# Opening and tail of a fused attention and mixture-of-experts kernel: first pairs' maxima by an accumulated product, keys of the first batch stored first, second block's attention reordered, last scatters unblocked

## The reference, cut to what matters

```python
# x: (4, 1024, 256), ctx: (4, 77, 256)
q = split(layernorm(x) @ W_q.T + b_q); k, v = split(ctx @ W_k.T + b_k), split(ctx @ W_v.T + b_v)
x = x + tanh(g0) * (merge(softmax(q @ k.T / 4) @ v) @ W_o.T + b_o)
h = layernorm(x) * ln_g + ln_b
top_vals, idx = top_k(h @ Wr, 2);  gates = softmax(top_vals)
shared = (silu(h @ W1s) * (h @ W3s)) @ W2s
# expert e takes its first 732 tokens, in order of choice and token
routed[t] += gate * ((silu(xe @ W1[e]) * (xe @ W3[e])) @ W2[e])
out = x + tanh(g1) * (routed + shared)
```

## Time and profile before

| | |
|---|---|
| median of 3 runs | 852.79 us (852.49 to 857.55) |
| the profiled execution | 850.94 us |
| its span | 849.2 us |
| TensorE busy | 97% of the span |

### The profile page before, as it was taken

One profiled execution on the slowest core, in us unless ns is written; L12 is line 12 of the kernel. 1 busy time (PEld: TensorE's weight loads), 2 busy tenths in 40 slices (PEclk: granted clock), 3 DMA queues, 4 the chain that ended last, 5 costly groups with the idle time before them and its releaser, 6 DMA issues.

```text
span 849.2 us, 14564 instructions
## 1 busy us (share of the span) xinstructions
PE 821.0 (97%) x5228; PEld 719.8 (85%) x5228; DVE 588.6 (69%) x1260; ACT 386.2 (45%) x660; POOL 321.6 (38%) x250
## 2 busy tenths in 40 slices
PE   8888999999999999999999999999999999999995
PEld 7474868868868688687788899999999999999995
DVE  7577788787788777888877666565656756566442
ACT  4547263373453633734445454453544545354331
POOL 7453103150032230303126405818275481834336
PEclk9999999999999999999999999999999999999998
DMA  8541411324104223130032624334444324431112
GB/s 265 136 125 28 125 38 35 90 53 119 19 25 124 43 52 85 34 100 14 26 125 53 194 75 108 71 83 105 110 88 88 102 46 112 98 76 17 16 25 38
DMA packets 92257, 67.24 MB, mean 79 GB/s; under 512 B 53556, under 2 KB 78984, under 8 KB 92200
## 3 DMA queue, kind: packets, MB, share of 16 engines
q1 hardware_dynamic: 39608, 54.79, 23.1%
q0 software_dynamic: 51744, 10.67, 8.8%
q10 hardware_dynamic: 848, 1.05, 0.5%
HBM read 37.75 MB, written 14.27 MB: 61 GB/s over the span
## 4 chain that ended last, share of the span: by engine, by line
PE 81%; DVE 4%; issue 3%; ACT 1%; POOL 1%; DVEq 0%; POOLq 0%; ACTq 0%
PE bank L1692 20%; PE bank L1694 20%; PE bank L1693 20%; PE bank L1993 3%; PE bank L1994 3%; PE bank L1995 3%; PE bank L1832 2%; PE bank L1826 2%; PE bank L1793 2%; PE bank L2035 1%; PE bank L1931 1%; PE bank L2019 1%; PE bank L1699 1%; PE bank L1922 1%; PE bank L1700 1%
## 5 line engine op out<-in xcount | busy, mean ns | idle before, releaser
L1692 PE MATMUL bank<-split_operands 128*128 128x366 f32 (+4 forms) x1104 | 364.9, 331 | 1.6 <-POOL split_operands L972 0.9
L1694 PE MATMUL bank<-split_operands 128*128 128x366 f32 (+4 forms) x1104 | 359.6, 326 | 0.0
L1693 PE MATMUL bank<-split_operands 128*128 128x366 f32 (+4 forms) x1104 | 359.5, 326 | 0.0
L1692 PEld LDWEIGHTS bank<-split_operands 128*128 128x128 f32 (+1 forms) x1104 | 205.8, 186 | 17.7 <-issue 5.9
L1694 PEld LDWEIGHTS bank<-split_operands 128*128 128x128 f32 (+1 forms) x1104 | 205.5, 186 | 10.6
L1693 PEld LDWEIGHTS bank<-split_operands 128*128 128x128 f32 (+1 forms) x1104 | 206.0, 187 | 8.1
L1084 POOL DMA_INDIRECT out<-float_data,scatter_now x42 | 120.1, 2860 | 170.1 <-DVE float_data L1655 146.7
L1675 DVE TENSOR_TENSOR hidden<-bank,float_data 128x366 f32<-128x366 f32 x112 | 60.5, 540 | 108.3 <-PE bank L1694 108.0
L1270 ACT ACTIVATE float_data<-bank 128x366 f32<-128x366 f32 x112 | 53.5, 477 | 110.2 <-PE bank L1694 110.2
L1267 ACT CAST split_operands<-hidden 128x366 fp32r<-128x366 f32 x112 | 55.7, 497 | 68.5 <-DVE hidden L1675 68.5
L1046 POOL DMA_INDIRECT float_data<-z_scratch,gather_now x42 | 72.9, 1736 | 17.6 <-issue 16.1
(11 more groups left out here) (177 smaller groups left out, 1116.1 us busy)
## 6 DMA issues: line engine op xcount, KB each, us to landing
float_data<-in_L_ffn_W SPq DMA_DIRECT2D x21, 1024.0 KB, 7.8
split_operands<-split_operands SPq DMA_DIRECT2D x92, 128.0 KB, 2.4
float_data<-in_x SPq DMA_DIRECT2D x8, 512.0 KB, 4.4
z_scratch<-float_data SPq DMA_DIRECT2D x8, 512.0 KB, 3.1
out<-float_data SPq DMA_DIRECT2D x7, 512.0 KB, 2.9
split_operands<-split_operands SPq DMA_DIRECT2D x8, 192.0 KB, 3.8
float_data<-in_L_ffn_W1s SPq DMA_DIRECT2D x2, 512.0 KB, 9.4
float_data<-in_L_ffn_W3s SPq DMA_DIRECT2D x2, 512.0 KB, 7.6
```

The costliest lines, as they stand in the source:

```text
L1692: pe.matmul(o, lhs[0], rhs[0], start=first, stop=False)
L1693: pe.matmul(o, lhs[0], rhs[1], start=False, stop=False)
L1694: return pe.matmul(o, lhs[1], rhs[0], start=False, stop=last)
```

## The change

It has four places.

**Opening, block 0.** Pairs 0 and 1 get their scores from two products into the same bank: one over the 96 rows of queries and keys, one of a constant `neg` (16 rows, -1 for the own head) with `mtr` itself. They don't wait for `mtr` to be broadcast by DMA. `neg` is made by GpSimd near the start. The key store is cut into the 77 columns of batch 0 and the rest, under two semaphores. ScalarE issues all eight DMAs of the queries' high parts, where SyncE issued four. The transposition of block 1's `xn` stands behind `first_scores`, and VectorE makes both of its parts. `scale_x` of block 1 stands behind `values_out`. Pieces 4 and 5 of the shared weights stand behind `scores(b, 1)`, high and low part.

**Block 0's z and block 1's z.** ScalarE makes the full value too (`full`), VectorE only subtracts (`low_z`); in block 0 VectorE does so behind both reductions of block 1's maxima.

**Block 1's attention.** VectorE scales block 2's `xn` behind the first half of the normalisation, not ahead of it. Its transposition stands ahead of `up(3)`, which stands ahead of the projection. `project_second` orders the projection's matmuls by what is ready: high parts of tiles 0 to 2, then their low parts, then tile 3. Four of six `keep_busy` matmuls go. An activation with no use for its result puts the table for Silu in place early. `up(6)` and `down(4)` are cut into parts around the maxima.

**Tail.** GpSimd no longer waits for `rows_gathered` in `rows_of_last`; VectorE's own wait for it stays.

```diff
     do("stack_maxima", b)
-    do("shared_hi", 2, 3)
+    do("values_out")
     do("scale_x", n)
-    do("shared_lo", 0, 1)
-    do("values_out")
-    do("shared_lo", 1, 6)
+    do("shared_lo", 0, 4)
...
+    do("shared_hi", 2, 3)
+    do("shared_lo", 4, 6)
...
-    nxt("scale_x")
     do("hidden", f, 2)
     nxt("keys")
     do("scores", b, 0)
+    nxt("scale_x")
     do("scores", b, 1)
+    do("silu_table")
+    nxt("transpose_x")
     up(3)
     do("attention_hi", b)
-    nxt("transpose_x")
     do("project", b)
...
             for j in range(2):
-                sp.dma_start(kscr[j].rearrange("(k p) t -> p k t", p=P), k_s[:, j].bitcast(F32)).then_inc(sig["k_stored"], 16)
+                sp.dma_start(kscr[j, :, 0:SK].rearrange("(k p) t -> p k t", p=P), k_s[:, j, :, 0:SK].bitcast(F32)).then_inc(sig["k0_stored"], 16)
+            for j in range(2):
+                sp.dma_start(kscr[j, :, SK:].rearrange("(k p) t -> p k t", p=P), k_s[:, j, :, SK:].bitcast(F32)).then_inc(sig["k_stored"], 16)
...
+            do(pool.memset(neg.bitcast(F32), 0.0))
+            first = neg.rearrange("p a b t -> p (a b) t")
+            pool.affine_select(out=first, in_=first.bitcast(F32), compare_op=ALU.not_equal, fill=-1.0, base=0,
+                               pattern=[[-1, 4], [0, SK]], channel_multiplier=1).then_inc(sig["neg_ready"], 1)
...
-            pool.wait_ge(sig["rows_gathered"], 16 * (NR // 2))
...
+        def full(b, k):
+
+            if b.at(1):
+                act.wait_ge(sig["hl_ready"], b.n * KD + k)
+            act.activation(full_of(b, k), bank[z_bank(b) + k][:, :], ACT.Identity, bias=lnb[:, k:k + 1],
+                           scale=lng[:, k:k + 1]).then_inc(sig["hf_ready"], 1)
...
         def transpose_x(b):
+            if b.at(1):
+                for k in range(KD):
+                    dve.wait_ge(sig["xT_ready"], KD + k + 1)
+                    dve.tensor_copy(xT[:, 0, k], bank[xT_bank(b) + k][:, :]).then_inc(sig["xh_ready"], 1)
...
         def pair_scores(b, p):
             for w in range(2):
+                if b.at(0) and p < 2:
+                    pe.matmul(bank[2 * (p % 2) + w][0:SK, :], kst[0:96, p, w, :], qst[0:96, p, :], start=True, stop=False)
+                    mm = pe.matmul(bank[2 * (p % 2) + w][0:SK, :], neg[:, p, w, :], mtr[:, :], start=False, stop=True)
+                    continue
...
+        def project_second(b):
...
+            pe.wait_ge(sig["ah_ready"], (b.n + 1) * KD)
+            high(0)
+            pe.wait_ge(sig["xl_ready"], (b.n + 2) * KD)
+            for t in (1, 2):
+                high(t)
+            pe.wait_ge(sig["al_ready"], (b.n + 1) * KD)
+            for t in range(3):
+                low(t)
+            pe.wait_ge(sig["x1_ready"], b.n * TT + 1)
+            high(3)
+            low(3)
```

More of the change, by code:

```diff
@@ L205, in second_period @@
     nxt("maxima", 1)
-    up(6)
+    do("up_a", f, 6)
+    down(4, 0, 1)
     nxt("maxima", 2)
-    down(4)
+    do("up_b", f, 6)
+    down(4, 1, 2)
     nxt("maxima", 3)
     do("pick", b, 1)
+    down(4, 2, TT)
     down(5)
@@ L1889, in project_first, with high, low @@
                     mm.then_inc(sig["oproj_ready"], 1)
+        def project_second(b):
+            aT, w = q_of(b), [wat[:, j, 3] for j in range(2)]
+            out = [bank[project_bank(b, t)][:, 0:D] for t in range(TT)]
+            at = [slice(t * P, (t + 1) * P) for t in range(TT)]
+            def high(t):
+                for k in range(KD):
+                    for j in range(2):
+                        pe.matmul(out[t], aT[:, 0, k, at[t]], w[j][:, k], start=(k + j == 0), stop=False)
+            def low(t):
+                for k in range(KD):
+                    mm = pe.matmul(out[t], aT[:, 1, k, at[t]], w[0][:, k], start=False, stop=(k == KD - 1))
+                mm.then_inc(sig["oproj_ready"], 1)
+            pe.wait_ge(sig["ah_ready"], (b.n + 1) * KD)
[9 more added lines that the diff above has]
+            low(3)
         def project(b):
```

79 lines of the change are left out of this document (49 added, 30 removed).

## The result

The changed kernel took **857.09 us** (median of 20 runs, 855.72 to 861.78), the kernel before 852.52 (20 runs, 850.52 to 860.12): a ratio of 1.0049, 95% interval 1.0031 to 1.0067. It is 4.6 us slower, where 3.2 us faster was forecast, and outside the range. The profiled execution took 855.82 us with a span of 854.1.

A forecast was written before the change was run, and what follows sets the result against it. TensorE, busy 821.0 of 849.2 us, was taken as the bound, leaving 28 us to gain. Terms +1.0 - 2.7 - 0.3 - 1.2 = -3.2 us gave 849.6 against the median of 852.79, range 846.8 to 854.5.

The forecast's parts named there:

- 2.8 us later, at 25.0: Opening: the keys' last load, issued near 22.2, lands at 25.0, so first scores start 3.3 us earlier than 28.29.
- the 0.15 us for the added issues ahead of four casts: Opening: ScalarE's four added DMA issues, 2.8 us, delay `mtr` by only 0.15 us, to 24.35.
- The four added matmuls double a row of 1.15 us to 2.3: Opening, first scores on TensorE: the added matmuls take the row from 1.15 to 2.3 us.
- the clock's fall at z alone: Rival, chance 0.22: TensorE's clock falls before block 0's z, costing 3.0 us more, 852.6 us in all.
- The norm starts at 51.1: Block 0, GpSimd: late pieces delay the loads of W2s, so the norm starts 0.9 us later than before.
- late weights: Rival, chance 0.10: loads of W2s take 7.6 us, not 3.9, and the clock's 3.0 come on top: 856.3 us.
- the rival by which GpSimd isn't the bound: Chance 0.12: loads land in 3 us, pieces run through, the norm starts near 49: 847.5 us in all.
- Net -2.7 us: Block 1, up to 87.18: idle time and `keep_busy` go, less short waits; -2.7 us, bounds -1.5 and -3.6.
- -0.3 behind it: `up(6)` and `down(4)` in parts let two reductions pass under matmuls: -0.3 us, bounds 0 and -0.5.
- -0.6, not -5: Tail: VectorE's last result sets the last scatter, at 840.7 instead of 841.34, though the first adding scatter starts 5 us earlier.
- -1.2 in sum: Tail: 0.6 us from the last scatter's earlier start, another 0.6 from faster landing, bounds 0 and 1.6.
- The opening was put at +1.0: Sum up to behind block 0's norm: 1.0 us slower, bounds -1.5 and +5.

The follow-up runs named there:

- e1: Changed kernel with SyncE again issuing four of the eight DMAs of the queries' high parts: 857.58 us, ratio 1.0048.
- t1: Kernel before with only the tail's edit, GpSimd not waiting for `rows_gathered`: 851.46 us, ratio 1.0000.
- t4: Kernel before with only ScalarE issuing all eight DMAs of the queries' high parts: 851.94 us, ratio 0.9997.
- g1: Kernel before with block 1's and the tail's edits and all eight DMAs of the queries' high parts on ScalarE: 847.08 us, ratio 0.9901.
- t2: Kernel before with only block 1's edits, the full value of z on ScalarE, and `up(6)` and `down(4)` cut: 850.00 us, ratio 0.9972.
- t3: Kernel before with block 1's and the tail's edits, so the change without its opening: 848.31 us, ratio 0.9942.
- e2: Changed kernel with seventeen `keep_busy` matmuls ahead of the first scores instead of three: 854.45 us, ratio 1.0005.
- e4: Changed kernel with seventeen `keep_busy` matmuls ahead of the first scores and pieces 4 and 5 ahead of the attention: 848.62 us, ratio 0.9940.
- e3: Changed kernel with pieces 4 and 5 of the shared weights ahead of the attention, as before: 851.76 us, ratio 0.9975.
- g3: e4 with the separate `neg` product taken away, pairs 0 and 1 waiting for the broadcast again: 847.25 us, ratio 0.9910.
- h3: Changed kernel with only the separate `neg` product taken away, `keep_busy` and pieces as they were: 853.79 us, ratio 1.0006.

## Why the prediction was wrong

**Which views were right.** That four waits stand where the profile shows them, and that each edit takes its wait away, held. The forecast fell on what takes their place in the opening.

**"Lands 2.8 us later, at 25.0": failed.** The keys were costed from rows in which nothing else ran beside them. Three things added up to 27.72: the opening was 0.5 us late from `neg` (costed at nothing), the six issues took 5.57 us instead of 4.3, and the last landed 3.15 us behind the end of its issue. e1 shows that 1.9 us of it are from ScalarE's added transfers beside them. `mtr` was there at 25.5, not 24.35: the 0.15 us for the added issues ahead of four casts was 0.7. The wait of 0.7 us for the store is gone, but that is no gain of the edit: without it t1, t4 and g1 start the loads at 18.4 to 18.6, and t2 and t3 at 19.1.

**"The four added matmuls double a row of 1.15 us to 2.3": failed, and it was the costly step.** It assumed the clock of the earlier trace rows. I placed the clock's fall at z alone and gave it 0.22; it came at both places. Eight matmuls took 5.07 us, the transposition 1.6. The change also leaves three of eight `keep_busy` matmuls ahead of the scores and none of the four behind them, to which I gave no price (e2, with seventeen ahead, takes back 2.6 us). The argument against a fall, that the level had stayed at 1.00 through 1.44 and 1.48 us of idle time, was from one execution: t1 shows the same opening with the level at 0.50. The Trainium skill (TensorE: Matmul & The Clock Gate, Part 1: The HAM clock gate) says that an idle TensorE loses half its rate. The trace agrees: 1.8 us into the 2.89 us without a matmul the level went from 1.00 to 0.50. An idle TensorE doesn't account for the falls of e1, e4 and t2, which came while it was busy.

**"The norm starts at 51.1": right in its mechanism, and well sized.** From the end of the attention to the norm I forecast 4.3 us more than before; it was 3.8 (W2s to ScalarE's cast 3.3 us, not 3.9). It came on top of an opening 3.5 us late instead of 3.4 early. With the second fall of the clock (0.8 us up to `up(1)`, where the rival had 3.0) the late pieces cost 5.3 us by e3. With them left in place (e3) the changed kernel is about level with the kernel before (0.9975, 0.9952 to 0.9999). The rival that came nearest in number, late weights at 856.3, isn't what happened: the loads of W2s landed in 4.0 us, not 7.6. And the rival by which GpSimd isn't the bound had a slip in its sum: with a load of 3.0 us the same chain gives 50.1 for the norm, not 49.

**"Net -2.7 us" in block 1 and -0.3 behind it: the sum held.** Up to block 2's queries it is -1.7. VectorE's stretched instruction is one of the reasons that it isn't more:

```profile
83.51 2.39 DVE L1363 TENSOR_SCALAR float_data<-float_data,mean_var,rstd 128x256 f32<-128x256 f32 x4
```

The scaling took 1.38 us before, and is now beside GpSimd's low part of 1.27 us (84.48), so that the transposition waits 0.46 in its middle. This microsecond isn't new: before, the same low part lay beside a normalisation (78.52), which took 1.39 us where its like takes 0.43. The projection waits 0.62 and 0.20. Behind the queries it is -1.0: the starts of t3 against those of before gain 0.3 at the two maxima, as forecast, and 0.4 between 224 and 246 us, where I had no term. Together -2.7 against -3.0, and t2 alone measured -2.5 by the medians and -2.0 at like clock.

**"-0.6, not -5" in the tail, -1.2 in sum: the size held, in part by luck.** The span shows -0.6; the runs of like clock -1.0 to -1.4. But the path was another one. VectorE's last result doesn't set the last scatter: it is there at 845.25, and the scatter starts at 846.51. The first of the last three scatters starts at 842.48, when VectorE is done with the tile of that time (842.43), and GpSimd issues the two others 2.0 us apart behind it. Against TensorE's end the last scatter came 0.3 us earlier, not 0.6, and the other 0.3 us lie behind its start.

**Signs.** Sum of the parts that were right: -3.3 us. The opening was put at +1.0 with bounds -1.5 to +5; it was +8.1. What failed there is that the clock was a rival of the forecast, with late keys in none of the cases, while the late keys made the gap in which it fell.

## What to carry to other kernels

A matmul that takes the place of a wait is not free because TensorE was idle there: count it at both levels of the clock, and count as work what merely keeps TensorE busy ahead of it. Before a step is moved behind another, follow what it releases (here the weights' load, through a semaphore that counts pieces), since that wait is paid in series later. And where medians of a change and of the kernel before spread over 10 us, compare executions by their mean granted clock; the parts that were worth keeping (block 1, tail, the issues moved to ScalarE) add up to 847.1 us, 5.1 us under the kernel before at like clock.

## What the runs showed of the hardware

The granted clock fell to 0.50 with TensorE busy too. In e1 it fell near 27.8, 2.0 us after a wait of 0.92 us had ended. In t2 it fell near 34.3, 2.1 us after a wait of 1.28 us had ended, with score matmuls over 112 rows ahead of it. In e4 it fell between 31 and 32, behind eight score matmuls of 0.38 us each that use 77 columns over 96 and 16 rows, with 0.27 us of idle time since 24.0. With four matmuls over 112 rows in their place (g3) it stayed at 1.00, and the mean of all nine runs is 0.996 or 0.997, where e4's ten have 0.992 to 0.997, five of them 0.997. Which of these things makes it fall isn't shown.

More transfers on ScalarE's queue lengthen the landing of SyncE's: with four of ScalarE's (six kernels) the keys' loads landed in 2.8 to 3.1 us, with eight (eleven kernels) in 3.8 to 4.6. The time to issue the six loads shows no such rule: 4.3 to 5.2 us with four, 4.15 to 5.9 with eight.

GpSimd's instructions lengthen VectorE's beside them: four scalings took 1.66 or 1.67 us in the ten kernels without `neg` beside them and 2.25 or 2.26 in the seven with it; 1.38 became 2.39 beside a low part of 1.27 us, and 0.43 became 1.39 for one multiplication. The Trainium skill (GPSIMD Engine Reference, 1. Specifications) says that the two share their access to SBUF; the traces agree.

What stays open: why the clock falls in e1, e4 and t2 with TensorE busy, why a fall lasts 3.4 us in h3, t3 and e4, some 10 in the changed kernel and 20 in e1 and t1, and why one program (the kernel before, t1, t4) has it in some executions and not in others.
